# A message stage of a graph network: gathered rows added by VectorE, shorter pieces, three rooms instead of six

## The reference

```python
ef = relu(edge_attr @ We1 + be1) @ We2 + be2        # 400000 x 128
ef = ef * sigmoid(ts @ Wt + bt)
combined = concatenate([x[row], ef], axis=1)        # x[row]: gathered rows
msg = relu(combined @ Wn1 + bn1) @ Wn2 + bn2
out = segment_sum(msg, col, num_segments=x.shape[0])
return out + x
```

## Time and profile before

| | |
|---|---|
| time, median of 3 runs | 8275.95 us (8274.34 to 8285.98) |
| time of the profiled execution | 8290.47 us |
| its span, first to last instruction | 8288.8 us |
| TensorE busy (matmul) | 6509.1 us, 79% |
| VectorE busy | 4750.7 us, 57% |
| ScalarE busy | 2462.6 us, 30% |
| GpSimd busy | 5925.0 us, 71% |
| granted TensorE clock, mean | 0.899 |

### The profile page before, as it was taken

How to read it: one execution, slowest core, us unless ns; L and a number is a source line. 1 busy time by engine, 2 the same in 40 slices (tenths; PEclk the granted TensorE clock), 3 DMA queues, 4 the chain that set the end, 5 groups by cost and what they waited for, 6 DMA issues and landing times.

```text
span 8288.8 us, 106834 instructions
## 1 busy us (share of the span) xinstructions
PE 6509.1 (79%) x34084; PEld 4100.4 (49%) x34084; DVE 4750.7 (57%) x8573; ACT 2462.6 (30%) x2998; POOL 5925.0 (71%) x5857
## 2 busy tenths in 40 slices
PE   5778777777776788887678888878888888888887
PEld 4555555444444555555444444444444444444444
DVE  8988877676755555555354444444444444444454
ACT  2111111111111000000134444444444444444444
POOL 7777665555547777777577777777777777777776
PEclk8889888888888999898799999999999999999998
DMA  4466666676758889898644444444444444444443
GB/s 122 154 201 223 228 231 227 232 240 219 249 190 285 290 298 309 303 318 305 216 124 125 130 127 127 129 123 128 126 128 126 129 127 130 125 128 129 128 129 98
DMA packets 598838, 1523.91 MB, mean 184 GB/s; under 512 B 157137, under 2 KB 290917, under 8 KB 587014
## 3 DMA queue, kind: packets, MB, share of 16 engines
q1 hardware_dynamic: 411075, 1133.17, 40.2%
q0 software_dynamic: 187200, 383.76, 16.7%
HBM read 1374.92 MB, written 141.47 MB: 183 GB/s over the span
## 4 chain that ended last, share of the span: by engine, by line
POOL 37%; issue 11%; PE 1%; DMA 1%; DVE 0%; POOLq 0%; ACT 0%; SPq 0%; DVEq 0%; ACTq 0%
POOL messages_rows L1704 37%; DMA messages_rows<-y_d,src_idx 1%; PE messages_p_msg L1785 1%; PE messages_p_msg L1788 0%; POOLq L1701 0%; DMA messages_sums<-in_message_base 0%; PE messages_win L1743 0%; PE messages_win L1761 0%; PE messages_win L1544 0%; DVE messages_below L1905 0%; DVE messages_parts L1895 0%; PE messages_p_edge L1800 0%; DVE messages_piece_stats L1559 0%; ACT messages_product L1833 0%; ACT L1536 0%
## 5 line engine op out<-in xcount | busy, mean ns | idle before, releaser
L1704 POOL DMA_INDIRECT messages_rows<-y_d,src_idx x3125 | 3190.2, 1021 | 1001.1 <-issue 944.5
L1110 POOL DMA_INDIRECT sum_x_rows<-in_x,sum_x_edges x1525 | 1568.5, 1029 | 855.8 <-PE sum_x_win L1200 428.3
L1900 DVE SCALAR_TENSOR_TENSOR messages_gated<-messages_p_edge,be,messages_gate 128x1024 f32<-128x1024 f32 x391 | 502.0, 1284 | 2138.8 <-PE messages_p_edge L1800 1039.3
L1110 POOL DMA_INDIRECT sum_z_rows<-z_d,sum_z_edges x1200 | 1165.0, 971 | 473.5 <-issue 419.2
L1785 PE MATMUL messages_p_msg<-messages_rows,identity 128*128 128x512 f32 x1564 | 963.2, 702 | 630.1 <-DMA messages_rows<-y_d,src_idx 611.5
L1788 PEld LDWEIGHTS messages_p_msg<-Wm_e,messages_gated 128*128 128x128 f32 x6250 | 937.6, 215 | 454.5 <-issue 454.5
L1212 PE MATMUL sum_x_build<-sum_x_key_hot,sum_x_low_hot 128*128 128x490 bf16 (+2 forms) x2900 | 837.0, 375 | 228.6 <-DVE sum_x_counts L1408 223.9
L1788 PE MATMUL messages_p_msg<-Wm_e,messages_gated 128*128 128x128 f32 x6250 | 929.2, 298 | 0.0
L1232 PE MATMUL sum_z_p_loaded<-sum_z_split,sum_z_counts 128*128 128x384 bf16 x2744 | 790.9, 346 | 155.1 <-DMA sum_z_split<-z_parts_d 149.9
L1820 ACT ACTIVATE messages_parts<-messages_p_msg 128x1024 bf16<-128x1024 f32 x391 | 399.7, 1022 | 1572.1 <-PE messages_p_msg L1788 1572.1
L1408 DVE SCALAR_TENSOR_TENSOR sum_x_counts<-sum_x_counts,sum_x_build 128x980 f32 (+3 forms) x635 | 647.8, 1020 | 360.6 <-PE sum_x_build L1212 348.5
(11 more groups left out here) (274 smaller groups left out, 9360.5 us busy)
## 6 DMA issues: line engine op xcount, KB each, us to landing
sum_x_split<-x_parts_d SPq DMA_DIRECT2D x392, 675.5 KB
sum_z_split<-z_parts_d SPq DMA_DIRECT2D x392, 675.5 KB
messages_when<-in_edge_weight SPq DMA_DIRECT2D x391, 512.0 KB
messages_attr<-in_span_attr SPq DMA_DIRECT2D x391, 256.0 KB, 3.1
counts_d<-sum_x_counts SPq DMA_DIRECT2D x28, 3136.0 KB
sum_z_counts<-counts_d SPq DMA_DIRECT2D x56, 1568.0 KB, 7.7
messages_rows<-y_d,src_idx POOLq DMA_INDIRECT x3125
sum_x_rows<-in_x,sum_x_edges POOLq DMA_INDIRECT x1525
```

What stands on the lines that cost most here:

```text
L1110: nc.gpsimd.indirect_dma_start(out=rows[:, s % depth, j, :], out_offset=None, in_=table, in_offset=bass.IndirectOffsetOnAxis(ap=edges[:, b ...
L1704: nc.gpsimd.indirect_dma_start(out=rows[:, g % SPAN_DEPTH, j, :], out_offset=None, in_=d["y"], in_offset=bass.IndirectOffsetOnAxis(ap=src_ ...
L1900: nc.vector.scalar_tensor_tensor(gated[:, g % SPAN_GATEDS, :], p_edge[:], t.be2[:, 0:1], gate[:, g % SPAN_GATES], ALU.add, ALU.mult).then_ ...
```

## The change

All of it lies in the message stage.

- TensorE no longer multiplies the rows by the identity, and no longer waits for rows. It lays `gated @ Wm_e` into the bank alone.
- VectorE waits for the rows and for that product, and adds the rows to the bank in place, 1024 columns at once. This stands in its slot after the last part of group s-3 and ahead of the gating of group s-1. ScalarE's first part and GpSimd's rooms wait for this addition (`msg_added`).
- The last part (L1895) and the one-hot (L1909) are made in pieces of two tiles (128x256), four for a full group, as tensor_tensor instead of scalar_tensor_tensor. Only the last piece signals.
- `rows` has three rooms of eight tiles in place of six.

```diff
-SPAN_DEPTH, SPAN_PARTS, SPAN_HOTS = 6, 3, 3
+SPAN_DEPTH, SPAN_PARTS, SPAN_HOTS = 3, 3, 3
-SPAN_SPACING, SPAN_SOON, SPAN_CHECK = 3, 16, 12
+SPAN_SPACING, SPAN_SOON, SPAN_CHECK, SHORT = 3, 16, 12, 2
...
-                wait_for(pool, msg_summed, g - SPAN_DEPTH + 1)
+                wait_for(pool, msg_added, g - SPAN_DEPTH + 1)
...
-                    before = sum(16 * tiles_of(i) for i in range(g % SPAN_DEPTH, g + 1, SPAN_DEPTH))
-                    pe.wait_ge(rows_arrived[g % SPAN_DEPTH], before)
-                    for h in range(0, tiles_of(g), 4):
-                        bank = range(h, min(h + 4, tiles_of(g)))
-                        nc.tensor.matmul(p_msg[:, bank[0] * P:(bank[-1] + 1) * P], t.identity[:],
-                                         rows[:, g % SPAN_DEPTH, bank[0]:bank[-1] + 1, :].rearrange("p j f -> p (j f)"), start=True, stop=False)
-                        for j in bank:
-                            last = nc.tensor.matmul(p_msg[:, j * P:(j + 1) * P], gated[:, g % SPAN_GATEDS, j * P:(j + 1) * P], t.Wm_e[:],
-                                                    start=False, stop=j == bank[-1])
+                    for j in range(tiles_of(g)):
+                        last = nc.tensor.matmul(p_msg[:, j * P:(j + 1) * P], gated[:, g % SPAN_GATEDS, j * P:(j + 1) * P], t.Wm_e[:],
+                                                start=True, stop=True)
                     last.then_inc(msg_summed, 1)
...
-                    act.wait_ge(msg_summed, g + 1)
+                    act.wait_ge(msg_added, g + 1)
...
-                    nc.vector.scalar_tensor_tensor(part(g, 2), below_of(g), 1.0, part(g, 1), ALU.mult, ALU.subtract).then_inc(low_ready, 1)
+                    for j in range(0, tiles_of(g), SHORT):
+                        own = slice(j, min(j + SHORT, tiles_of(g)))
+                        last = nc.vector.tensor_tensor(part(g, 2)[:, own], below_of(g)[:, own], part(g, 1)[:, own], ALU.subtract)
+                    last.then_inc(low_ready, 1)
+                for g in groups(s, SPAN_MSG_LAG):
+                    before = sum(16 * tiles_of(i) for i in range(g % SPAN_DEPTH, g + 1, SPAN_DEPTH))
+                    dve.wait_ge(rows_arrived[g % SPAN_DEPTH], before)
+                    dve.wait_ge(msg_summed, g + 1)
+                    nc.vector.tensor_tensor(message(g), message(g), rows[:, g % SPAN_DEPTH, 0:tiles_of(g), :], ALU.add).then_inc(msg_added, 1)
...
-                    n = tiles_of(g)
                     wait_for(dve, win_summed, g - SPAN_HOTS + 1)
-                    nc.vector.scalar_tensor_tensor(
-                        hot[:, g % SPAN_HOTS, 0:n], t.iota[:].unsqueeze(1).to_broadcast([P, n, P]), 1.0,
-                        rel[:, g * SPAN:g * SPAN + n].unsqueeze(2).to_broadcast([P, n, P]), ALU.mult, ALU.is_equal).then_inc(hot_ready, 1)
+                    for j in range(0, tiles_of(g), SHORT):
+                        n = min(SHORT, tiles_of(g) - j)
+                        last = nc.vector.tensor_tensor(
+                            hot[:, g % SPAN_HOTS, j:j + n], t.iota[:].unsqueeze(1).to_broadcast([P, n, P]),
+                            rel[:, g * SPAN + j:g * SPAN + j + n].unsqueeze(2).to_broadcast([P, n, P]), ALU.is_equal)
+                    last.then_inc(hot_ready, 1)
```

More of the change, by code:

```diff
@@ L1664, in sum_messages @@
     gate_ready, gated_ready = sem("gate_ready"), sem("gated_ready")
-    msg_summed = sem("msg_summed")
+    msg_summed, msg_added = sem("msg_summed"), sem("msg_added")
     high_ready, rest_ready, middle_ready, low_ready = sem("high_ready"), sem("split_rest_ready"), sem("middle_ready"), sem("low_ready")
```

## The result

The changed kernel takes 8141.7 us, the median of four runs (8134.5 to 8144.4), against 8279.5 for the kernel before (8274.3 to 8286.0): ratio 0.9832, 95% interval 0.9815 to 0.9849, 138 us less. Forecast were 8135 us and a range of 8095 to 8215. The profiled execution took 8141.5 us, its span is 8139.6.

The account below looks back on a forecast made before the run. GpSimd's gathers, never resting, were taken to bound the kernel. Short pieces -139, rooms +3 and the end -5 gave -141 us: 8149.5 us profiled, less 14.5 for the runs' median, 8135 us; range 8095 to 8215.

Parts of the forecast that it names:

- What bounds the kernel: Message stage: GpSimd's gathers never rest, 1.32 us each, 10.6 us per group; VectorE operations with two SBUF inputs lengthen some.
- Short pieces: Last part and one-hot in four pieces each: gather excess falls from 237 to 98 us, -139 us.
- two premises under it: Gathers start at random moments of VectorE's 1.25 us cycle; a held gather waits only for one instruction's end.
- Rival 1: Queued pieces of a series leave no opening and hold a gather as one: 8373 us, chance 0.05.
- Rows added by VectorE: VectorE's message-bank addition replaces TensorE's identity matmuls: about 1.2 us per group, its contention with gathers priced at nothing.
- Rival 3: TensorE falls to its lower clock level; granted mean near 0.6 uses up the gain; chance 0.04 slower, 0.03 no change.
- Rooms: GpSimd's wait with three rooms: none in steady work, +3 us in slot 8; 8 to 11 if VectorE's block is not earlier.
- The end: After the last gather, message matmuls no longer stand behind the rows: -5 us, bounds 0 and -6.
- Sum: Whole kernel: -139 + 3 - 5 = -141 us, 8149.5 us profiled, 8135 us for the runs' median.
- Rival 2: In last part and one-hot, tensor_tensor does not hold a gather, so all 237 us go: 8037 us, chance 0.04.

Follow-up runs that it names:

- memset above: The addition alone kernel with a useless VectorE memset of 128x640 (about 0.6 us) put ahead of each one-hot: 8690.2 us, ratio 1.0497.
- addition alone: The changed kernel with last part and one-hot as single 128x1024 operations again, VectorE's addition and three rooms kept: 8358.0 us, ratio 1.0106.
- pieces alone: The kernel before with only the pieces of one-hot and last part; TensorE still adds rows, six rooms: 8149.0 us, ratio 0.9844.
- one-hot first: The changed kernel with the one-hot's pieces moved ahead of the addition in VectorE's order: 8120.4 us, ratio 0.9816.

## Why the prediction was right

- **What bounds the kernel** was right: GpSimd's gathers, without rest, before and after. L1897, with one input in PSUM, held nothing, and in steady work what held had two inputs in SBUF (the one-hot and the last part). The rule of the Trainium skill ("SBUF — State Buffer", section "Who interferes with whom"), by which a VectorE instruction with two SBUF inputs contends with GpSimd's reads, agrees with both. Two SBUF inputs are not the only thing that holds a gather, though. The memset above has no input at all and takes part in holds, and in slot 8 of the kernel with the addition alone a cast with one SBUF input held a gather until 0.81 us after its end (4176.14):

```profile
4174.42 1.72 DVE L1836 CAST messages_sums<-messages_sums 128x2997 f32<-128x2997 int32 x1
4174.93 2.02 POOL L1704 DMA_INDIRECT messages_rows<-y_d,src_idx  x1 [0.30 <-issue]
```

- **Short pieces**, forecast -139 us: the holds fell from 237 to (972 - 944) x 3125 = 87.5 us, so -149.5. Forecast were 98 us left, with 70 to 117 as bounds. A piece took 419 ns and a series 1.42 us, as forecast (0.42 and 1.41).
- **The two premises under it** were weaker than its number. The first, that gathers start at random in VectorE's work, fails where operations are long: the same two operations held 0.61 us per group before and 0.83 with the addition. Starts are not random in the changed kernel either: of 399 gathers that began while a one-hot's series ran, 117 began 0.2 to 0.3 us after its start. Pieces bound a hold by their length, and so the estimate came near. That it came as near as 0.22 us per group against 0.25 is in part luck, since the same pieces held 0.26 in the kernel with the pieces alone and 0.18 with the one-hot first. The second premise, that every end of an instruction is an opening, holds in the changed kernel in all but 14 cases, and fails with one-tile pieces. Rows 9 already spoke against it: the gather of 4188.84 ended at 4192.23, 1.75 us after the end of the cast that it met. Rival 1 (pieces hold as one), to which I gave 0.05, is not how this change went, but the thing exists: the kernel with one-tile pieces loses 186 us against the changed one, by holds over the last part's series.
- **Rows added by VectorE**, forecast no cost: L1897 took 1233 ns (forecast 1215 to 1284), VectorE was busy 2406/(2939/8) = 6.55 us per group (6.6), and additions waited for rows, 963 us. With long operations, though, this part costs 84 us, by holds that grow with the phase that it sets. It is free in this change only because the pieces stand beside it.
- **TensorE** fell to 2794/(2939/8) = 7.6 us per group at a granted 0.85 (forecast 7.1 and 0.8 to 0.87), so its work was put 0.5 us too low, off the path. Rival 3 did not come about: the clock went from 0.94 to 0.85 and the time did not notice.
- **Rooms**, forecast +3 us: 0.8 us. VectorE's block lay at 4183 to 4210, 5 us earlier as forecast, and the addition ended at 4212.8 (forecast 4213).
- **The end**, forecast -5 us: from the last gather's start to the end of the span 33.5 us became 30.0.
- **Sum**: forecast -141. The spans differ by 149.2 us (stage -148.4, end -3.5, and a stage start 2.7 us later), the medians by 138. Rival 2 is excluded by the 87.5 us of holds that remain.

## What to carry to other kernels

When GpSimd makes the descriptors of gathers and never rests, look at the longest gathers and at what VectorE did at their start: instructions with two SBUF inputs held them to their end, and a long cast did too. Cut such instructions short and, if they stand back to back, check in the trace that gathers pass between them; a wait of VectorE on its own piece, which left 0.035 us between two, made them pass here. It was worth 246 us with one-tile pieces, and that kernel is 60 us faster than the changed one, whose two-tile pieces have no waits. A part that is free by busy times can still set the phase of all that follows, so measure it without its neighbour.

## What was not expected of the hardware

- Eight instructions of 0.28 us in a row held a gather for up to all of them, 1.6 us, where four of 0.42 us nearly always let it through after the first. Only the last part did so; the one-hot's eight, of the same length, hardly ever.
- A 0.59 us memset right ahead of the one-hot made all 343 gathers that began shortly before or in it wait for the one-hot's end, while a memset of 2.56 us elsewhere held none.
- A kernel with more VectorE work (8.4 for 6.55 us per group) was 60 us faster, and one with a 0.59 us memset added per group 332 us slower, both by what happened to gathers alone.
- With two rooms GpSimd stood 2.0 to 3.9 us at every fourteenth group, with no releaser in the trace.
